# Gated delta attention on one core: a second set of split weights, small VectorE operations in two-operand form, and another order of work in the mixing loop

## What is computed

```python
qkv = silu(causal_conv4(layernorm(x) @ Wqkv));  z = xn @ Wz
q, k = l2norm(q), l2norm(k)                      # 16 heads, width 128
def step(M, inp):                                # along the 512 tokens
    M = M * exp(g_t)
    Mk = einsum('bhd,bhdv->bhv', k_t, M)
    M = M + einsum('bhd,bhv->bhdv', k_t, (v_t - Mk) * b_t)
    return M, einsum('bhd,bhdv->bhv', q_t, M)
out = rmsnorm(out) * norm_w * silu(z)
x = x + layernorm(out @ Wout);  x = x + layernorm(mlp(layernorm(x)))
```

## Time and profile before

| | |
|---|---|
| median of 3 runs | 2894.31 us (2894.02 to 2895.68) |
| the profiled execution | 2893.81 us, its span 2891.9 us |
| share of the span busy | PE 93%, DVE 78%, ACT 74%, POOL 65% |
| mean granted clock of TensorE | 0.975 |

### The profile page before, as it was taken

How to read it: one execution, slowest core, us unless ns; L and a number is a source line. 1 busy time by engine, 2 the same in 40 slices (tenths; PEclk the granted TensorE clock), 3 DMA queues, 4 the chain that set the end, 5 groups by cost and what they waited for, 6 DMA issues and landing times. The chain is left out here.

```text
span 2891.9 us, 70042 instructions
## 1 busy us (share of the span) xinstructions
PE 2690.6 (93%) x23604; PEld 2278.7 (79%) x23604; DVE 2257.9 (78%) x5006; ACT 2143.2 (74%) x7286; POOL 1892.7 (65%) x1706
## 2 busy tenths in 40 slices
PE   3399999999999999999999999999999999986998
PEld 2288888888888888888888888888888888873554
DVE  5588888888888888888888888888888888853433
ACT  2388888888888888788888887888888887861211
POOL 2267777777777777777777777777777777751000
PEclk9699999999999999999999999999999999997999
DMA  5322222222222222222222222222222222201100
GB/s 190 126 87 94 89 87 77 95 89 83 82 87 96 89 81 82 96 89 80 83 96 89 87 77 95 89 83 82 87 96 89 81 82 89 89 5 53 36 29 29
DMA packets 78567, 241.78 MB, mean 84 GB/s; under 512 B 8336, under 2 KB 21520, under 8 KB 61584
## 3 DMA queue, kind: packets, MB, share of 16 engines
q1 hardware_dynamic: 78224, 237.41, 23.3%
HBM read 223.75 MB, written 13.63 MB: 82 GB/s over the span
## 5 line engine op out<-in xcount | busy, mean ns | idle before, releaser
L744 DVE SCALAR_TENSOR_TENSOR conv<-pj,cw,conv 128x511 f32<-128x511 f32 (+2 forms) x1152 | 847.0, 744 | 54.6 <-ACT conv L619 40.5
L926 PE MATMUL pj<-xt,w_hi 128*128 128x512 f32 x2048 | 694.5, 421 | 23.1 <-DVE wo L738 23.1
L539 POOL TENSOR_TENSOR kq<-kq,cum 128x512 f32<-128x512 f32 x256 | 428.1, 1693 | 0.0
L926 PEld LDWEIGHTS pj<-xt,w_hi 128*128 128x128 f32 x2048 | 354.5, 193 | 70.2 <-DVE wo L738 23.5
L926 PE MATMUL pj<-xt,w_lo 128*128 128x512 f32 x1024 | 409.3, 400 | 0.0
L568 POOL TENSOR_TENSOR inv<-inv,x 128x512 f32<-128x512 f32 x128 | 148.1, 1157 | 379.0 <-ACT inv L678 379.0
L619 ACT ACTIVATE conv<-pj,cw 128x512 f32<-128x512 f32 x384 | 266.0, 693 | 143.6 <-PE pj L926 133.4
L818 DVE TENSOR_TENSOR y<-bk,mask 128x256 f16<-128x256 f32 x512 | 216.3, 422 | 167.8 <-PE bk L992 160.3
L575 POOL TENSOR_TENSOR attn<-attn,part 128x512 f32<-128x512 f32 x256 | 326.5, 1276 | 9.0 <-ACT part L701 9.0
L638 ACT ACTIVATE squares_out<-tr 128x128 bf16<-128x128 f32 x1024 | 273.0, 299 | 47.8 <-PE tr L933 47.8
L1072 PE MATMUL pj<-wo,yt 128*128 128x256 f32 x1024 | 282.6, 399 | 0.8 <-DVE yt L869 0.8
(11 more groups left out here) (159 smaller groups left out, 7559.3 us busy)
## 6 DMA issues: line engine op xcount, KB each, us to landing
xt<-xt_scratch SPq DMA_DIRECT2D x128, 1024.0 KB, 4.8
decay<-decay_scratch SPq DMA_DIRECT2D x128, 256.0 KB, 5.3
cum<-cumdecay_scratch SPq DMA_DIRECT2D x128, 256.0 KB, 5.5
w_raw<-in_w_heads SPq DMA_DIRECT2D x16, 512.0 KB, 3.4
xt_scratch<-xt_hi SPq DMA_DIRECT2D x8, 512.0 KB, 2.8
xt_scratch<-xt_lo SPq DMA_DIRECT2D x8, 512.0 KB, 3.8
res<-in_x SPq DMA_DIRECT2D x8, 512.0 KB, 4.8
out<-yo SPq DMA_DIRECT2D x8, 512.0 KB, 3.1
```

Of the source, the lines that this page charges most:

```text
L539: last = nc.gpsimd.tensor_tensor(part, part, of(cum, p)[:, :], ALU.mult)
L744: nc.vector.scalar_tensor_tensor(out=conv[:, i, j:SEQ], in0=pj[:, i % 2, 0:SEQ - j], scalar=cw[:, i, p // NSEQ, TAPS - 1 - j:TAPS - j], in ...
L926: last = nc.tensor.matmul(pj[:, i % 2, :], w[:, kt, cols], x_[:, kt, :], start=(n == 0), stop=(n == 3 * KT - 1))
```

## The change

1. `w_hi` and `w_lo` get two sets, used in turn by head. `split` of head h waits for the projections of head h-2, not h-1, and is issued in the slots 1, 3, 5 and 7 of the head before, behind `out_norm` on GpSimd; before, it stood in slots 7 (Q, K) and 0 (V, Z), at four places of the list.
2. Four small operations of VectorE (`norms`, `q_norm` and r0, and `state_scale`, which has two) are written as scalar_tensor_tensor. Where there is no second tensor it is the first again (`max` of s + EPS and s, `min` of s * EPS * P and s, which changes no value), or, for r0, a new tile of zeros.
3. The lists of all four engines have another order. `scale_k_tok` works on pair a-1 instead of a-2, `q_norm` on a-2 instead of a-1, `norms` and `convolve(V, 2)` stand at the start of the next step instead of the end of this one, and `solve(0)`, `state_input(0)` likewise. `outputs(0)` stands behind `solve(3)` instead of behind `solve(1)`.
4. `LAST_STAGE` is 5 instead of 4: one more iteration at the end, in which no pair is real.

```diff
-LAST_STAGE = 4
+LAST_STAGE = 5
...
-    w_hi = buf(ctx, "w_hi", [P, KT, 4 * P], F32R)
-    w_lo = buf(ctx, "w_lo", [P, KT, 4 * P], F32R)
+    w_hi = [buf(ctx, f"w_hi{i}", [P, KT, 4 * P], F32R) for i in range(2)]
+    w_lo = [buf(ctx, f"w_lo{i}", [P, KT, 4 * P], F32R) for i in range(2)]
...
+    zeros = buf(ctx, "zeros", [P, P])
...
                     cols = slice(P * i, P * i + P)
+                    hi, lo = w_hi[head % 2][:, :, cols], w_lo[head % 2][:, :, cols]
                     pool.wait_ge(w_in, DMA * (head + 1))
-                    wait(pool, proj[i], NSEQ * head)
-                    nc.gpsimd.tensor_copy(w_hi[:, :, cols], w_raw[:, :, cols]).then_inc(w_copied[i], 1)
+                    wait(pool, proj[i], NSEQ * (head - 1))
+                    nc.gpsimd.tensor_copy(hi, w_raw[:, :, cols]).then_inc(w_copied[i], 1)
...
-                if slot == 0 and head:
-                    split(V, head)
                 unit_diagonal(a - 1)
-                scale_k_tok(a - 2)
                 out_norm(a - 4)
-                if slot == NSEQ - 1:
-                    split(Q, head + 1)
+                if slot % 2:
+                    split(slot // 2, head + 1)
+                add(0, a - 4)
+                low_b(a - 1)
                 first_transpose(a - 1)
+                scale_k_tok(a - 1)
...
-                    nc.vector.tensor_scalar(of(k2, p)[:, :, :], of(sums, p)[:, :, :], EPS, None, ALU.add).then_inc(k2_ready, 1)
+                    nc.vector.scalar_tensor_tensor(out=of(k2, p)[:, :, :], in0=of(sums, p)[:, :, :], scalar=EPS,
+                                                   in1=of(sums, p)[:, :, :], op0=ALU.add, op1=ALU.max).then_inc(k2_ready, 1)
...
-                        nc.vector.tensor_scalar(r[:, 0, :], of(v_tok, p)[:, 0, :], of(kn, p)[:, 0:1], None,
-                                                ALU.mult).then_inc(r_ready[0], 1)
+                        nc.vector.scalar_tensor_tensor(out=r[:, 0, :], in0=of(v_tok, p)[:, 0, :],
+                                                       scalar=of(kn, p)[:, 0:1], in1=zeros[:, :],
+                                                       op0=ALU.mult, op1=ALU.subtract).then_inc(r_ready[0], 1)
```

More of the change, by code:

```diff
@@ L582, in _ @@
                 scale_b(a - 1)
-                if slot == 0 and head:
-                    split(V, head)
                 unit_diagonal(a - 1)
-                scale_k_tok(a - 2)
                 out_norm(a - 4)
-                if slot == NSEQ - 1:
-                    split(Q, head + 1)
+                if slot % 2:
+                    split(slot // 2, head + 1)
+                add(0, a - 4)
+                low_b(a - 1)
                 first_transpose(a - 1)
+                scale_k_tok(a - 1)
+                add(1, a - 4)
+                k_norm(a - 1)
                 scale_kq(a - 1)
[L592 to L598, removed]
                 inverse(a - 2)
-                add(0, a - 4)
         @block.scalar
@@ L727, in _ @@
                 convolve(V, a)
+                state_input(3, a - 3)
+                take(2, a - 1)
                 correction(a - 2)
                 squares(turned_k, 0, sums_k, a)
-                state_input(3, a - 3)
                 take_k(a)
-                state_input(0, a - 2)
         @block.vector
@@ L871, in _ @@
             for a in range(PAIRS + LAST_STAGE):
+                convolve(V, 2, a - 1)
                 convolve(V, 3, a - 1)
+                norms(a - 1)
+                inverse_norm(a - 1)
                 mask_level(3, a - 2)
-                inverse_norm(a - 1)
                 decay_b(a - 1)
@@ L923, in project @@
                     x_hi, x_lo = of(xt, p)[:, 0, :, :], of(xt, p)[:, 1, :, :]
+                    hi, lo = of(w_hi, p // NSEQ), of(w_lo, p // NSEQ)
                     for kt in range(KT):
-                        for w, x_ in ((w_hi, x_hi), (w_hi, x_lo), (w_lo, x_hi)):
+                        for w, x_ in ((hi, x_hi), (hi, x_lo), (lo, x_hi)):
                             last = nc.tensor.matmul(pj[:, i % 2, :], w[:, kt, cols], x_[:, kt, :],
@@ L1076, in _ @@
             for a in range(PAIRS + LAST_STAGE):
+                solve(0, a - 3)
                 outputs(3, a - 4, signal=o_done)
+                turn_v(a - 1)
                 state_update(0, a - 3)
                 tx_level(3, a - 2)
-                turn_v(a - 1)
+                from_state_k(1, a - 3)
+                turn_o(a - 4)
                 project(Z, a - 1)
-                from_state_k(1, a - 3)
+                out_project(0, a - 4)
                 z_level(4, a - 2)
-                turn_o(a - 4)
-                solve(1, a - 3)
-                out_bank_free(a - 3)
-                outputs(0, a - 3)
+                z_first(a - 1)
+                out_project(1, a - 4)
                 tx_level(4, a - 2)
-                z_first(a - 1)
-                out_project(0, a - 4)
-                state_update(1, a - 3)
+                project(Q, a)
                 z_level(1, a - 1)
                 z_level(5, a - 2)
-                out_project(1, a - 4)
+                solve(1, a - 3)
+                project(K, a)
+                state_update(1, a - 3)
                 tx_level(5, a - 2)
-                project(Q, a)
+                tx_level(1, a - 1)
+                out_bank_free(a - 3)
+                outputs(1, a - 3)
+                from_state_k(2, a - 3)
                 z_level(6, a - 2)
-                tx_level(1, a - 1)
-                from_state_k(2, a - 3)
-                project(K, a)
                 solve(2, a - 3)
@@ L1103, in _ @@
                 tx_level(6, a - 2)
-                outputs(1, a - 3)
-                tx_level(2, a - 1)
-                outputs(2, a - 3)
-                residual(a - 2)
+                turn_q(a)
                 state_update(2, a - 3)
-                turn_q(a)
                 project(V, a)
                 from_state_k(3, a - 3)
+                residual(a - 2)
+                tx_level(2, a - 1)
+                solve(3, a - 3)
+                outputs(0, a - 3)
+                turn_k(a)
                 correction(a - 2)
-                turn_k(a)
-                solve(3, a - 3)
+                outputs(2, a - 3)
                 grams(a)
-                solve(0, a - 2)
                 z_level(3, a - 1)
```

49 lines of the change are left out of this document (25 added, 24 removed).

## The result

The changed kernel takes 2900.01 us (median of 9 runs, 2898.12 to 2904.67), the kernel before 2894.32 (9 runs, 2891.41 to 2895.97): ratio 1.0022, 95% interval 1.0012 to 1.0032. So it is slower by 0.2%, by 5.7 us. The forecast was 2894 us, that is no change; of the three sides slower had been given 0.44, the same 0.33, faster 0.23. The time lies in the range. The nine runs lie in two clusters, 2898.1 to 2900.0 and 2902.1 to 2904.7 us, and the profile is of the fastest of them.

What follows compares the result with a forecast made beforehand. TensorE's queue was taken to bound the kernel; the heads' 67.4 us saved were given back as 127 x 0.53 = 67.3 us by a step of 19.18 us, so 2894 us, no change, with a range of 2866 to 2930.

Steps and rivals of the forecast that it cites:

- The bound: Ordinary step of 18.65 us: only TensorE's queue order and length count; the other three engines have 2 to 4 us free.
- The row of r0 with 1.15 us: VectorE's r0, held by GpSimd's b over the SBUF port, was expected to wait as before: 1.15 us.
- The head, 67.4 us: 15 head changes, 4.5 us each, from TensorE waiting for GpSimd's x; two weight sets were to remove all 67.4 us.
- The waits that go, 0.37 us a step: TensorE's L1033 weight loads waiting for r and inv; the new order was to remove 0.37 us, leaving 18.28.
- The switches: TensorE changes from 16-bit to 32-bit groups, 11 a step before, 10 after: taken as 0, range -0.1 to +0.05 us.
- Place one and two: TensorE stops before from_state_k(1) (behind m0) and solve(2) (behind r2): 0.33 and 0.57 us a step, slower pairs included.
- Neither stop can hide: TensorE runs its queue in order and nothing it could do stands between, so both new stops cost in full.
- 18.28 + 0.33 + 0.57 = 19.18: New step in us: step without waits plus the stops before from_state_k(1) and solve(2), 0.53 more than before.
- B: Rival: one thin cover (x, yt, v_tok or vt) is late by 0.3 us; step 19.33, +19 us, 2913; chance 0.26.
- C: Rival: GpSimd's out_norm power holds the port against VectorE's scan; step 19.76, +74 us, 2968; chance 0.07.
- D: Rival: pairs behind a wait not drawn out, dropped switch counts; step 18.98, -25 us, 2869; chance 0.18.
- E: Rival: the change doesn't free the head, 4.5 us stays at each head change; 2961 us; chance 0.05.

Runs made afterwards that it cites:

- experiment 5: Changed kernel with from_state_k(2) moved one place sooner on TensorE, ahead of outputs(1): 2903.72 us.
- experiment 6: Changed kernel with outputs(0) moved from behind solve(3) to between z_level(6) and solve(2): 2893.68 us.
- experiment 7: Kernel of experiment 3 with solve(1) one place later on TensorE, behind outputs(0): 2825.92 us, ratio 0.9763.
- experiment 3: Kernel before, in its old order, with two weight sets and each split (slots 1, 3, 5, 7) late in GpSimd's queue, ahead of inverse: 2829.22 us, ratio 0.9773.
- experiment 1: Kernel before, in its old order, with two weight sets and splits spread over slots 1, 3, 5, 7 behind out_norm: 2843.61 us, ratio 0.9824.
- experiment 8: Changed kernel with the small VectorE operations (norms, q_norm, state_scale, r0) back in their old forms: 2899.15 us.
- experiment 9: Changed kernel with GpSimd's scale_k_tok back at its old place, pair a-2, ahead of out_norm: 2915.92 us.

## Why the prediction was right or wrong

**The bound, right but too simple.** The order and length of TensorE's queue set the step. "The other three engines have 2 to 4 us of room" is true of their sums only: links of VectorE and ScalarE are within 0.1 us of TensorE at several places (experiments 5 to 7). The row of r0 with 1.15 us that the prediction read is one of two kinds (experiment 7); in the changed kernel it takes 0.87 us in 122 of 128 steps.

**The head, 67.4 us: right.** 66.0 in the loop of experiment 3. In the changed kernel the splits' place does no harm; a place two entries away in another order costs 0.25 us every second step (experiment 1).

**The waits that go, 0.37 us a step: mis-sized.** The one for r was real, 0.19 us (experiment 7). The one for inv was not: that weight load waited while grams ran, and grams moves the next start by 1.73 us in the kernel before, with this wait, and in the changed one, where its row has shrunk from 127 places to 2. So 0.18 too much was taken off. A waiting load (PEld) costs only what delays the next start.

**The switches, 0 with -0.1 as a bound: mis-sized the other way.** By TensorE's starts the old step is 18.66, and the new one without its stops 19.22 - 0.31 - 0.51 = 18.40. That is 0.26 less, of which 0.19 is r; the other 0.07 is what the reordered groups gained net of the two slower pairs (0.02 and 0.03), so 0.12 in all. That fits the prediction's own rows: one switch fewer, at 0.31 us against 0.21. It is read from starts and was not tested by itself.

**Place one and two: right.** Stops 0.31 and 0.51 against 0.30 and 0.54, pairs 0.33, round trips 0.77 and 0.89, all from two lines of the run-out. "Neither stop can hide" held too, more strongly than it was meant.

**The sum.** 18.28 + 0.90 = 19.18 was forecast, and the 124 steps behind the first take 19.21 at the median and 19.214 on average. So 0.18 too much gain at the waits stood against 0.12 too little at the switches and 0.03 too much cost at the stops. In the loop, 2436.6 us against the 2431.4 forecast, that is 124 x 0.034 = 4.2 us; the first step (17.66) is 1.5 us shorter than an ordinary step of the forecast, and the last two together 2.5 longer than its 33.91. They take 19.61 + 16.78 = 36.39 us at a clock of 0.85 and 0.87. That goes with the clock and not with a wrong saving: in the profile of experiment 8, with the same order on TensorE, they took 17.84 + 15.82 = 33.66 at a clock of 1.00, and the 30 us after them then ran at 0.60 where the changed kernel has 0.86. Why the clock falls at another time was not separated; nor was the 3.4 us later first residual group, beside which the stretch behind the last one is 4.3 us shorter.

So the step that failed is the netting in "18.28 + 0.33 + 0.57 = 19.18". The 0.37 us of waits taken off was 0.19, since the wait for inv cost nothing, and the switches put at 0 gave back 0.12. The two errors cancel for the most part, and that the time still came within 6 us is partly luck. Two terms of 67 us each were right to 1 and 4 us, and what is left between them is the verdict: a forecast of no change, and a kernel that is slower by 4.2 us in the profiled run (5.1 in the loop, 0.9 less outside it). The bounds of the switches alone (-0.1 to +0.05 a step, 19 us wide) were wider than the band called no change. They also give 2881 to 2900 us and not the 2887 to 2902 that the prediction printed for them.

**Rivals.** *B* (a thin cover tears) did not happen in the changed kernel: yt's load waits 22.9 us in the list, but out_project(0) follows the projection at the usual 0.23. It is near: x's cover tears in experiments 1 and 9, yt's in 7. *C* fell: the scan follows out_norm's power by 0.10 us and is not held,

```profile
1044.92 1.02 POOL L564 TENSOR_TENSOR oc<-oms,halves 128x4 f32<-128x4 f32 x1 [0.78 <-DVE oms L861]
...
1045.02 1.21 DVE L751 TENSOR_TENSOR_SCAN e<-decay,ident 128x512 f32<-128x512 f32 x1
```

while r0, in its two-operand form, is held by b to b's end:

```profile
1042.32 1.04 POOL L508 TENSOR_TENSOR b<-b,f 128x512 f32<-128x512 f32 x1 [1.82 <-DVE f L779]
...
1042.63 0.87 DVE L847 SCALAR_TENSOR_TENSOR r<-v_tok,kn,zeros 128x128 f32<-128x128 f32 x1
```

The Trainium skill (SBUF — State Buffer, Who interferes with whom) lets whoever is second wait until the first is done; r0 and x of experiment 1 agree with it, the scan beside the power does not. *D* fell in its first half (pairs of 0.33); its second half, the dropped switch, is in the 0.12. *E* fell (no step at a head is longer).

## What to carry to other kernels

Split a change into its terms and run them apart: here one edit was worth 66 us and the other cost 71, and the version without the reordering beats both kernels by over 2%. A stop behind a round trip between engines is not free room. Before you move a link or a filler to close it, list for each neighbour what it waits for and how long ago that was started, since the next link may open by the same amount; and read stops from the distance of starts: the list of waits shows some of them too short or not at all, and has rows that cost nothing. Look at more than one step before you take a length as typical.

## What the runs showed of the hardware

A round trip TensorE, VectorE, TensorE costs 0.77 us with a plain copy of 128x128 (0.87 in the run-out, where its first pair is drawn out by 0.10) and 0.89 us with a three-operand product, in the loop as in the run-out, as long as VectorE is free when the data come. A 512-column product of GpSimd that starts during VectorE's scan is held to the scan's end (2.09 us for 1.16), and one that starts beside r0 holds it or the 4-column q_norm behind it (1.15 or 1.00 us for 0.28 and 0.16), in the kernel before by turns; a GpSimd power of 4 columns takes 1.02 us and did not hold the scan beside it. Stops of 0.31 and 0.51 us in every step leave the granted clock at 1.00 through the loop. The granted clock of the last steps differs between two kernels with the same TensorE order (0.85 and 1.00), and the other way round in the 30 us behind them (0.86 and 0.60).
